# Left and right column halves of a float32 product taken in turn, so that consecutive matmuls use two PSUM banks

## The reference

```
h = gelu(cond @ W0 + b0); h = gelu(h @ W1 + b1)
att = softmax(h @ W2 + b2)                              # 128 x 8
y = einsum('boi,bih->boh', einsum('bk,koi->boi', att, weight), x) + (att @ bias_k)[:, :, None]
logits = y @ W_router.T                                 # 8 experts, top 2, renormalised
h = einsum('nd,erd->ner', y, A); expert_out = einsum('ner,eor->no', h * combine, B) * 2
out = x + y @ W_base.T + b_base + expert_out
```

## Time and profile before

| | |
|---|---|
| median of three runs | 980.33 us (979.67 to 981.19) |
| profiled execution, own time | 979.68 us |
| its span, first to last instruction | 978.0 us |
| mean granted TensorE clock (1 is 2.4 GHz) | 0.993 |
| PE busy | 949.5 us (97%), 6697 matmuls |
| DVE busy | 702.1 us (72%) |
| ACT busy | 331.3 us (34%) |
| matmuls of lines 369, 371 and 373 | 3 x 1792 = 5376 |

### The profile page before, as it was taken

One profiled execution on the slowest core, in us unless ns is written; L12 is line 12 of the kernel. 1 busy time (PEld: TensorE's weight loads), 2 busy tenths in 40 slices (PEclk: granted clock), 3 DMA queues, 4 the chain that ended last, 5 costly groups with the idle time before them and its releaser, 6 DMA issues.

```text
span 978.0 us, 18969 instructions
## 1 busy us (share of the span) xinstructions
PE 949.5 (97%) x6697; PEld 941.9 (96%) x6697; DVE 702.1 (72%) x1560; ACT 331.3 (34%) x663; POOL 90.3 (9%) x134
## 2 busy tenths in 40 slices
PE   6889999999999999999999999999999999999995
PEld 4779999999999999999999999999999999999994
DVE  4896767777676777777687767677776767777774
ACT  4442333333233333333333323333332333333331
POOL 0200101011010101001010101010110101010010
PEclk9999999999999999999999999999999999999998
DMA  5444434443434444343434444343444344443424
GB/s 206 168 136 127 107 113 122 98 109 113 129 94 125 96 115 117 110 127 92 131 88 109 122 119 107 112 123 97 109 113 129 92 126 97 113 118 110 126 51 106
DMA packets 35084, 112.45 MB, mean 115 GB/s; under 512 B 13024, under 2 KB 13280, under 8 KB 30464
## 3 DMA queue, kind: packets, MB, share of 16 engines
q1 hardware_dynamic: 25856, 78.73, 22.0%
q0 software_dynamic: 9216, 33.56, 20.4%
HBM read 76.56 MB, written 35.65 MB: 115 GB/s over the span
## 4 chain that ended last, share of the span: by engine, by line
PE 92%; DVE 4%; DMA 2%; ACT 1%; issue 1%; SPq 0%; DVEq 0%
PE ps L371 24%; PE ps L369 24%; PE ps L373 24%; PE ps L417 9%; PE ps L394 3%; PE ps L395 3%; PE ps L396 3%; DMA w_stage<-in_wide 1%; DVE w_lo L834 1%; PE ps L430 1%; ACT w_hi L581 1%; DMA result<-x_sb 1%; DVE w_stage L838 1%; DVE b_stage L838 0%; DVE x_sb L823 0%
## 5 line engine op out<-in xcount | busy, mean ns | idle before, releaser
L369 PE MATMUL ps<-w_hi,x_hi 128*128 128x290 f32 x1792 | 539.7, 301 | 9.2 <-DVE w_lo L834 4.4
L371 PE MATMUL ps<-w_lo,x_hi 128*128 128x290 f32 x1792 | 535.0, 299 | 0.0
L373 PE MATMUL ps<-w_hi,x_lo 128*128 128x290 f32 x1792 | 533.5, 298 | 0.0
L369 PEld LDWEIGHTS ps<-w_hi,x_hi 128*128 128x128 f32 x1792 | 340.4, 190 | 13.0 <-issue 9.5
L371 PEld LDWEIGHTS ps<-w_lo,x_hi 128*128 128x128 f32 x1792 | 340.8, 190 | 0.0
L373 PEld LDWEIGHTS ps<-w_hi,x_lo 128*128 128x128 f32 x1792 | 340.5, 190 | 0.0
L546 ACT CAST x_hi<-xT_sb 128x512 fp32r<-128x512 f32 x192 | 119.0, 621 | 193.5 <-DVE xT_sb L754 168.9
L738 DVE TENSOR_TENSOR x_lo<-xT_sb,x_hi 128x512 fp32r<-128x512 f32 x192 | 131.4, 686 | 37.7 <-ACT x_hi L546 37.7
L719 POOL DMA_DIRECT2D x_sb<-in_x x64 | 56.3, 880 | 522.3 <-DVE x_sb L828 522.1
L814 DVE TENSOR_TENSOR hwT_lo<-ps,hwT_hi 128x128 fp32r<-128x128 f32 x64 | 18.7, 292 | 101.8 <-ACT hwT_hi L558 101.0
L561 ACT COPY sum<-ps 128x580 f32<-128x580 f32 x96 | 61.8, 643 | 65.5 <-PE ps L373 64.7
(11 more groups left out here) (84 smaller groups left out, 893.5 us busy)
## 6 DMA issues: line engine op xcount, KB each, us to landing
x_sb<-in_x POOLq DMA_DIRECT2D x64, 512.0 KB, 5.3
result<-x_sb SPq DMA_DIRECT2D x64, 512.0 KB, 2.7
xT_sb<-in_xT SPq DMA_DIRECT2D x31, 1024.0 KB, 4.8
w_stage<-in_wide SPq DMA_DIRECT2D x3, 1160.0 KB, 6.6
agg_w_rows<-agg_w SPq DMA_DIRECT2D x1, 2048.0 KB, 8.6
mix<-agg_w_rows SPq DMA_DIRECT2D x124, 16.0 KB, 3.9
w_stage<-in_wide SPq DMA_DIRECT2D x2, 580.0 KB, 7.6
b_stage<-in_wide SPq DMA_DIRECT2D x1, 1160.0 KB, 13.5
```

The lines of the kernel that those rows point to most:

```text
L369: nc.tensor.matmul(dst, x_hi[:, s, rows], w_hi[:, w, c, cols], start=first, stop=False, skip_group_check=True)
L371: nc.tensor.matmul(dst, x_hi[:, s, rows], w_lo[:, w, c, cols], start=False, stop=False, skip_group_check=True)
L373: mm = nc.tensor.matmul(dst, x_lo[:, s, rows], w_hi[:, w, c, cols], start=False, stop=last, skip_group_check=True)
```

## The change

The two parts of a product are no longer taken one after the other. For each chunk and each of the three operand pairs both parts are taken in turn, so that consecutive matmuls have the same stationary operand and go to the banks `bank` and `bank + 1` alternately. The number of matmuls, their shapes, their operands and, in each bank, the order of additions are as before. In the loop, where A12 and S3 have a transpose in their middle, the transpose stands after both parts of chunks 0 and 1 and no longer after all chunks of part 0.

```
-            def product_part(bank, name, part, start, chunks=slice(0, CHUNKS)):
-                dst, cols, s, w = ps[:, bank + part, 0:PART], slice(part * PART, (part + 1) * PART), SLOT[name], WEIGHT[name]
+            def product_chunks(bank, name, start, chunks=slice(0, CHUNKS)):
+                dsts = [ps[:, bank + part, 0:PART] for part in range(2)]
+                cols = [slice(part * PART, (part + 1) * PART) for part in range(2)]
+                s, w = SLOT[name], WEIGHT[name]
                 for c in range(chunks.start, chunks.stop):
                     rows, last = slice(c * P, (c + 1) * P), c == CHUNKS - 1
                     first = start and c == 0
-                    nc.tensor.matmul(dst, x_hi[:, s, rows], w_hi[:, w, c, cols], start=first, stop=False,
-                                     skip_group_check=True)
-                    nc.tensor.matmul(dst, x_hi[:, s, rows], w_lo[:, w, c, cols], start=False, stop=False,
-                                     skip_group_check=True)
-                    mm = nc.tensor.matmul(dst, x_lo[:, s, rows], w_hi[:, w, c, cols], start=False, stop=last,
-                                          skip_group_check=True)
+                    for part in range(2):
+                        nc.tensor.matmul(dsts[part], x_hi[:, s, rows], w_hi[:, w, c, cols[part]], start=first, stop=False,
+                                         skip_group_check=True)
+                    for part in range(2):
+                        nc.tensor.matmul(dsts[part], x_hi[:, s, rows], w_lo[:, w, c, cols[part]], start=False, stop=False,
+                                         skip_group_check=True)
+                    for part in range(2):
+                        mm = nc.tensor.matmul(dsts[part], x_lo[:, s, rows], w_hi[:, w, c, cols[part]], start=False,
+                                              stop=last, skip_group_check=True)
                 return mm
...
-                for part in range(2):
-                    mm = product_part(a, "A11", part, True, js)
+                mm = product_chunks(a, "A11", True, js)
...
-                product_part(b, "A12", 0, True)
+                product_chunks(b, "A12", True, slice(0, 2))
                 transpose_hw(u - 1, 0)
-                product_part(b, "A12", 1, True).then_inc(product_mm, 1)
+                product_chunks(b, "A12", True, slice(2, 4)).then_inc(product_mm, 1)
...
-                product_part(a, "S3", 0, False)
+                product_chunks(a, "S3", False, slice(0, 2))
                 transpose_hw(u - 1, 1)
-                product_part(a, "S3", 1, False).then_inc(product_mm, 1)
+                product_chunks(a, "S3", False, slice(2, 4)).then_inc(product_mm, 1)
```

More of the change, by code:

```diff
@@ L368, in product_part @@
                     first = start and c == 0
-                    nc.tensor.matmul(dst, x_hi[:, s, rows], w_hi[:, w, c, cols], start=first, stop=False,
-                                     skip_group_check=True)
-                    nc.tensor.matmul(dst, x_hi[:, s, rows], w_lo[:, w, c, cols], start=False, stop=False,
-                                     skip_group_check=True)
-                    mm = nc.tensor.matmul(dst, x_lo[:, s, rows], w_hi[:, w, c, cols], start=False, stop=last,
-                                          skip_group_check=True)
+                    for part in range(2):
[7 more added lines that the diff above has]
+                                              stop=last, skip_group_check=True)
                 return mm
             def product(bank, name, start):
-                for part in range(2):
-                    mm = product_part(bank, name, part, start)
-                mm.then_inc(product_mm, 1)
+                product_chunks(bank, name, start).then_inc(product_mm, 1)
             def column_sums(bank, w, start=False, stop=False):
```

## The result

The changed kernel takes 986.13 us in the median of six runs (984.17 to 987.17), the kernel before 980.34 us beside it (979.26 to 982.22). The ratio is 1.0055, with a 95% interval from 1.0042 to 1.0068: slower by 0.55%, 5.4 us (the two medians lie 5.8 us apart). The forecast was no change, 980.3 us, with a range of 977.5 to 984.5.

What follows compares the result with a forecast made beforehand. TensorE was taken to bound the kernel, by the number of matmuls and their pace. 978.0 us span + 1.7 us around it = 979.7 us, plus 0 us of change; forecast median 980.3 us, range 977.5 to 984.5 us.

Steps and rivals of the forecast that it cites:

- PE bounds, its waits and clock stay, the transposes and the tail cost nothing.: Whole kernel: PE busy 97% of the span, clock 1.00 from 75 us on, no wait added; cost 0.
- The rival of a clock in bursts: Loop units: 1.4 us at the 1.2 GHz level in each of 31, +43 us, 1024 us; chance 0.03 with other losses.
- writes in two banks: Product matmuls: alternating banks hide the surcharge of adding to the predecessor's bank, about 909 us, half 944; chance 0.04.
- The experts' block is very nearly the pattern of the change, hence 0 ns.: Expert matmuls change banks every time and pay 13.3 ns like products, so an added bank change costs 0 ns.
- all combinations but one: Trace blocks by bank and stationary operand: only four equal stationary operands in a row, together with other banks, is lacking.
- The surcharge is 13.3 ns.: Product matmuls: 134.2 ns each, less 120.8 ns for 290 columns, leaves 13.3 ns beyond the columns.
- A change of bank costs about a nanosecond: about 985 us.: Products, 4928 added bank changes: 0.9 to 1.1 ns each, +4.4 to +5.4 us; chance 0.08.
- the 48 matmuls: Two products between an expert and a mixing block: 6.44 us if right, 6.49 if a bank change costs 1 ns.
- The bounds of ±5.4 us: Added bank changes: 1.1 ns more or less each by expert and mixing readings, times 4928.

Runs made afterwards that it cites:

- the crossed kernels: New operand order with the banks of the kernel before: 985.12 us; old operand order with the changed kernel's banks: 980.86 us.
- theory P: Follow-up theory, no run: a matmul's distance to the next depends on the phase in which the matmuls before it left TensorE; units settle into repeating patterns.
- aligned_before: Kernel before with each moving slice started at the next lower multiple of 64 bytes, result not the reference's: 980.62 us, ratio 1.0001.
- the added one with 32 columns: Kernel before with one more matmul of 32 columns in each unit, ahead of A11: 983.71 us, ratio 1.0032.

## Why the prediction was wrong, point by point

- *PE bounds, its waits and clock stay, the transposes and the tail cost nothing.* Right: no new wait, clock 1.00, 31 like units (but for one wait of 0.6 us in the loop's second, 1.0 us after). The rival of a clock in bursts did not occur: PE changed banks at every product matmul and the granted clock stayed at 1.00. The Trainium skill, page "TensorE: Matmul & The Clock Gate", section "A second HAM failure mode: psum-queue depth-cycling", tells of a kernel in which TensorE idled between groups of matmuls; by the rows here the change of banks alone brings neither the idling nor the lower clock. Nor was there anything to gain from writes in two banks (unit 28.768 us with them alone).
- *"So the question is what a matmul's surcharge depends on: the bank of its predecessor, or the stationary operand of its predecessor."* This is the step that failed. There is a third thing that the change moves, the sequence of slices on the moving side, and it alone carries the loss; both things that I named have no effect to a nanosecond (unit 28.768 with new banks, 28.769 with new stationary operands). The 0 ns for a change of bank was right. What failed is that the surcharge was carried over unchanged, a term put at nothing because the moving slices were not looked at: it grew by 0.174 us a unit, 0.8 ns for each of 206 matmuls. The claim that the trace held "all combinations but one" was made over the wrong two variables.
- *The experts' block is very nearly the pattern of the change, hence 0 ns.* It is like the change in its banks, which do not matter. Its stationary operand was misread: `hwT_hi` stays for six matmuls in a row, one change inside nine and not one in three. So it was wrong, too, that no block of the trace has four equal stationary operands in a row; this one has six and the column sums have 24. Its moving slices are another sequence with other widths, so its 13.3 ns said nothing on the products' new sequence. The block even changed itself, from 1.408 to 1.42 us, because of what streamed ahead of it.
- *The surcharge is 13.3 ns.* It is a mean of unlike distances. The kernel before had 3257 ns for S2 and 3203 for S4, the same shape and the same order of banks. This was to be seen: S2 is the row at 593.50 us, with mixing behind it at 596.75, 3.25 us, while S4 and A22 take 6.44 together, 3.22 each in the mean.

```profile
593.50 0.29 PE L369 MATMUL ps<-w_hi,x_hi 128*128 128x290 f32 x1
...
596.75 0.34 PE L394 MATMUL ps<-z_hi,mix_hi 128*128 128x384 f32 x1
```

  Equal work that differs by 1.7% without a wait says that a hidden variable is at play of the size of the whole question: 54 ns by 224 products are 12 us.
- *A change of bank costs about a nanosecond: about 985 us.* The time came out near (986.13), and the 48 matmuls took the 6.49 us (6.50) that this rival gave. The agreement is chance: the crossed kernels show a price of zero. The signature chosen for it could not tell it from another cause that adds a nanosecond.
- *The range.* The bounds of ±5.4 us reached 985.7, and the range was cut at 984.5, within the far part of a rival that had a chance of 0.08. The uncertainty of the pace was larger than those rows could show.

What stays open is the mechanism. Shown is that of the three things the change moves, the sequence of moving slices alone makes the difference, and that slice starts and widths change its size and its sign. Shown too is that a unit's time depends on more than its own instructions, since in one kernel equal units without a wait took 28.68 and 28.76 us. Why one sequence settles at 28.77 us and another at 28.94 was not found; no rule tried here (fixed price for halves in turn, starts at 64 bytes, groups of 16 columns, the same slice twice) foretells it. That distances depend on a phase, which was part of theory P, is neither shown nor excluded. Whether the reads and writes of DVE, ACT and the DMAs in the same memories have a part was not tried.

## What to carry to other kernels

In this kernel, with TensorE full, reordering matmuls made a unit up to 0.6% longer at 290 columns and 0.4% shorter at 288, and the number of instructions, banks and stationary operands did not tell which. Reckon with as much where TensorE is full. Before calling a surcharge constant, compare like blocks in the trace; if equal blocks differ by more than the effect in question, the forecast needs at least that width. And cross the variables of an edit in pairs of kernels, even with a meaningless result: four runs separated banks, stationary operands and slices here, while a signature that several causes share would have confirmed the wrong one.

## What was not expected of the hardware

- With PE full, distances repeat to a nanosecond or so: in the kernel before, 28 of 29 successive units took 28.766 or 28.767 us, and each of the 24 distances in S2 is the same in every unit to 1 ns, while among themselves they lie between 128 and 145 ns.
- The repeating lengths are near multiples of 6.667 ns (16 cycles at 2.4 GHz): 28,766.6 (4315 of them are 28,766.7), 28,940 (4341), 28,833.3 (4325), 28,880.0 (4332), 28,873.3 (4331). In aligned_before the length repeats only over three units (28.787, 28.827, 28.826), while the loop's code repeats over two; the three together, 86.440 us, are 12,966 times 6.667 ns. A period that the code doesn't have says that something is carried over from one unit to the next. The cause was not tried.
- A matmul with a weight load of its own took at least about 0.11 us here: the added one with 32 columns 0.113 us, the transpose of `hw` with 128 columns 0.113 us (28 ns to the next start, which is then itself 85 ns late) and 0.109 us in the changed kernel, an expert matmul with 248 columns 0.113 us.
- Accumulating into the same bank again and again costs nothing against changing it: one bank for twelve matmuls and a new bank at each gave the same unit to the nanosecond (28.768 us in both).
